# Shorter score tiles for the early queries of a cross attention, and constants made later, in a one-core decoder layer

## The reference

```python
def _L0_xattn_ref(x, encoder_output, mask, WQ, WK, WV, WO):   # H = 16, DK = 8
    q, k, v = ...                                             # (b, h, 64, 8)
    scores = jnp.einsum('bhqd,bhkd->bhqk', q, k) / SQRT_DK
    future = jnp.triu(jnp.ones((s, s), jnp.int32), 1)
    m = mask[:, None, :, None] + future[None, None, :, :]     # the mask is by query
    scores = jnp.where(m != 0, NEG, scores)
    attn = jax.nn.softmax(scores, axis=-1)
    return jnp.einsum('bhqk,bhkd->bqhd', attn, v)... @ WO
x = _layernorm(x + _L0_attn_ref(x, ...))
x = _layernorm(x + _L0_xattn_ref(x, ctx_1024, mask, ...))
x = _layernorm(x + _L0_ffn_ref(x, ...))
```

## Time and profile before

| | us |
|---|---|
| median of 3 runs | 600.04 |
| lowest and highest | 596.92, 603.64 |
| the profiled execution | 602.87 |
| its span | 601.2 |
| busy: PE, DVE, ACT, POOL | 527.9, 416.3, 369.0, 330.8 |

### The profile page before, as it was taken

How to read it: one execution, slowest core, us unless ns; L and a number is a source line. 1 busy time by engine, 2 the same in 40 slices (tenths; PEclk the granted TensorE clock), 3 DMA queues, 4 the chain that set the end, 5 groups by cost and what they waited for, 6 DMA issues and landing times.

```text
span 601.2 us, 22996 instructions
## 1 busy us (share of the span) xinstructions
PE 527.9 (88%) x9312; PEld 370.4 (62%) x9312; DVE 416.3 (69%) x1453; ACT 369.0 (61%) x643; POOL 330.8 (55%) x603
## 2 busy tenths in 40 slices
PE   2699998989999999988999999998989989999741
PEld 1467776656677767755666666666646656666530
DVE  2567777766767765375587778777867787779743
ACT  2356566557777777766766666666656666666520
POOL 6766667745755556341337554655465447554563
PEclk9899999999999999999999999999999999999876
DMA  5610000000000001001112111111111011111001
GB/s 160 188 38 3 3 1 2 3 3 1 1 2 1 2 5 26 1 11 28 27 32 49 29 40 33 49 30 43 29 48 28 27 48 50 28 34 22 20 19 35
DMA packets 24986, 17.97 MB, mean 30 GB/s; under 512 B 3120, under 2 KB 21424, under 8 KB 24880
## 3 DMA queue, kind: packets, MB, share of 16 engines
q1 hardware_dynamic: 24448, 16.43, 10.4%
q10 hardware_dynamic: 432, 0.07, 0.1%
HBM read 9.67 MB, written 4.19 MB: 23 GB/s over the span
## 4 chain that ended last, share of the span: by engine, by line
PE 58%; SPq 9%; ACT 8%; DVE 7%; issue 7%; POOL 6%; DMA 4%; POOLq 0%; DVEq 0%; ACTq 0%
SPq L394 8%; PE pair L1145 7%; PE pair L1179 7%; PE pair L1194 6%; PE pair L1213 6%; PE pair L1258 5%; PE pair L1114 5%; PE pair L1223 4%; PE pair L1036 4%; DMA k_exp<-k_sb 3%; ACT gel L718 3%; PE pair L1107 3%; PE pair L1232 2%; PE pair L1201 2%; PE pair L1049 2%
## 5 line engine op out<-in xcount | busy, mean ns | idle before, releaser
L718 ACT ACTIVATE gel<-pair 128x1024 f32<-128x1024 f32 x64 | 65.5, 1024 | 75.4 <-PE pair L1213 75.4
L926 DVE TENSOR_REDUCE neg_max<-pair 128x16 f32<-128x1024 f32 x64 | 60.9, 951 | 20.3 <-PE pair L1201 20.2
L1194 PE MATMUL pair<-k_exp,qT 64*32 64x256 f32 (+1 forms) x1024 | 57.5, 501 | 8.5 <-DMA k_exp<-k_sb 7.7
L1179 PEld LDWEIGHTS pair<-w,gel 128*128 128x128 f32 x512 | 60.3, 192 | 7.4 <-issue 5.5
L1223 PEld LDWEIGHTS pair<-v,gel 128*32 128x32 f32 x4096 | 41.7, 110 | 37.1 <-ACT gel L718 31.2
L1179 PE MATMUL pair<-w,gel 128*128 128x128 f32 x512 | 62.2, 276 | 1.0 <-ACT gel L643 1.0
L1223 PE MATMUL pair<-v,gel 128*32 128x18 f32 x4096 | 48.2, 187 | 15.5 <-ACT gel L718 12.8
L1145 PE MATMUL pair<-hT,w 128*128 128x512 f32 x128 | 58.5, 597 | 1.9 <-ACT lev L638 1.3
L712 ACT ACTIVATE gel<-gel,row_scale 128x512 f32<-128x512 f32 x80 | 54.4, 719 | 4.8 <-DVE gel L939 4.8
L303 POOL TENSOR_SCALAR veps_c<-mv_c 128x4 f32<-128x4 f32 x16 | 3.7, 229 | 96.0 <-issue 89.8
L303 POOL TENSOR_SCALAR veps_b<-mv_b 128x4 f32<-128x4 f32 x32 | 7.8, 245 | 81.6 <-DVE mv_b L295 45.8
(11 more groups left out here) (127 smaller groups left out, 1228.5 us busy)
## 6 DMA issues: line engine op xcount, KB each, us to landing
X<-in_x SPq DMA_DIRECT2D x16, 256.0 KB, 3.0
cT<-in_ctx SPq DMA_DIRECT2D x16, 256.0 KB, 2.9
out_rows<-X SPq DMA_DIRECT2D x16, 256.0 KB, 2.5
k_exp<-k_sb SPq DMA_DIRECT2D x160, 16.0 KB
w<-in_L_attn_w SPq DMA_DIRECT2D x2, 256.0 KB, 3.3
w_kv<-in_L_attn_wk SPq DMA_DIRECT2D x1, 64.0 KB, 3.2
w_q<-in_L_attn_wq ACTq DMA_DIRECT2D x1, 64.0 KB, 3.0
w_kv<-in_L_attn_wv SPq DMA_DIRECT2D x1, 64.0 KB, 3.1
```

The costliest lines, as they stand in the source:

```text
L718: nc.scalar.activation(pT[par], pair[par][:, :, :].rearrange("p a c -> p (a c)"), ACT.Copy).then_inc(pT_ready, 1)
L926: nc.vector.tensor_reduce(neg_max[par][:, :].rearrange("p (a h) -> p a h", a=2), scores, AX.X, ALU.max, negate=True).then_inc(max_ready, 1)
L1179: last = nc.tensor.matmul(bank(6 + q)[:, P * t:P * (t + 1)], gel[:, q, f, P * t:P * (t + 1)], w_2[:, f, :], start=(f == 0), stop=(f == NF ...
L1194: nc.tensor.matmul(pair[t % 2][b * QW:(b + 1) * QW, half, 0:HH * width], qT[p][rows, batch + first:batch + first + QW], keys, start=True, ...
```

## The change

- Odd tiles keep 32 keys per head to the end: probabilities of 512 columns, four transposes in place of eight, a copy of 512 columns, then four products of 144 columns (a masked query's share of the later 32 keys, from `future` and `v2`) and sixteen of 36 columns, from a new array `v4`. The even tiles add the causal term for the last 32 keys only (256 columns in place of 512).
- `v4` is a second copy of the values, which POOL writes in each group: `spread_v`, four copies, between `ln_b` and `ln_c` of its step. POOL's two `future_keys` per group go.
- `future` is made by DVE, one instruction per group (new `future_keys`), from rows of the mask that SP loads two groups ahead with one more DMA per group (`load_mask`), between the ten of `spread_k` and the load of the context. Two such loads follow the first context load.
- POOL's constants of the cross attention move from between `rows1` of groups 1 and 2 in stage one to behind the two `zero`, ahead of step 2 of `phase2`; those for `v4` and `late_key` are added.
- At the start of the cross attention ACT does `probabilities(0)` ahead of `rows_a(13)`, and `rows_a(14)` and `rows_a(15)` stand one and two slots later. `y2` takes the memory of `xn[0]` and `causal` that of `y2T`.

```diff
+            def load_mask(g, p):
+                src = mask_early[2 * g:2 * g + 2, :].rearrange("n p -> (n p)")
+                sp.dma_start(mask_rows[p][:, :, :].rearrange("p n q -> p (n q)"),
+                             src.partition_broadcast(P)).then_inc(mask_loaded[p], 16)
...
                 if exists(s + 2):
+                    if s >= 0:
+                        sp.wait_ge(future_ready, s + 1)
+                        load_mask(s + 2, p)
                     after(sp, xv_done, s + 1)
                     load_ctx(s + 2, p)
...
+            def late_constants():
+                const(nc.gpsimd.memset(causal, 0.0))
+                const(nc.gpsimd.memset(late_key[:, :], 0.0))
...
+                for i in range(2):
+                    const(nc.gpsimd.memset(v2[i][:, :, :, :, :], 0.0))
+                    for h in range(2):
+                        const(nc.gpsimd.memset(v2[i][h * S:(h + 1) * S, :, :, h, DH:HV], 1.0))
+                    const(nc.gpsimd.memset(v4[i][:, :, :, :, :], 0.0))
+                    for j in range(QB):
+                        const(nc.gpsimd.memset(v4[i][j * QW:(j + 1) * QW, :, :, j, DH:HV], 1.0))
+                    const(nc.gpsimd.memset(moe_out[i][:, :, 2 * D + NE:], LOWEST))
+                pool.sem_inc(const_ready)
...
-            def future_keys(m):
...
+            def spread_v(g, q):
+
+                pool.wait_ge(v2_ready, g + 1)
+                apart(pool)
+                heads = v2[q].rearrange("p u (i j) h e -> p u i j h e", j=2)
+                for j in range(2):
+                    for h in range(2):
+                        slot = 2 * j + h
+                        nc.gpsimd.tensor_copy(
+                            v4[q][slot * QW:(slot + 1) * QW, :, :, slot, 0:DH],
+                            heads[h * S:h * S + QW, :, :, j, h, 0:DH]).then_inc(v4_ready, 1)
+                        pool.wait_ge(v4_ready, g * QB + slot + 1)
...
             for s in range(2):
                 zero(k_exp[s])
 
+            late_constants()
             pipeline(pool, phase2, first=2, last=NG - 4)
...
-                nc.scalar.activation(pT[par], pair[par][:, :, :].rearrange("p a c -> p (a c)"),
-                                     ACT.Copy).then_inc(pT_ready, 1)
+                flat = pair[par][:, :, :].rearrange("p a c -> p (a c)")
+                nc.scalar.activation(pT[par], flat[:, 0:GW] if n % 2 else flat, ACT.Copy)\
+                    .then_inc(pT_ready, 1)
...
+            probabilities(0)
             rows_a(NG - 3, 1)
-            probabilities(0)
+            act.wait_ge(down_done, NG)
+            phase3(0, 0, slots=(0, 1))
             rows_a(NG - 2, 0)
-            act.wait_ge(down_done, NG)
-            phase3(0, 0, slots=(0,))
+            phase3(0, 0, slots=(2,))
             rows_a(NG - 1, 1)
-            phase3(0, 0, slots=range(1, TG))
+            phase3(0, 0, slots=(3,))
...
+            def future_keys(g, q):
+
+                dve.wait_ge(mask_loaded[q], g // 2 * 16 + 16)
+                after(dve, pv_done, g * TG - TG)
+                nc.vector.tensor_scalar(future[q][:, :, :], mask_rows[q][:, :, :], 0.0,
+                                        late_key[:, 0:1], ALU.not_equal, ALU.mult)\
+                    .then_inc(future_ready, 1)
...
-                for i in range(HH):
+                for i in range(HH // 2 if n % 2 else HH):
...
+                if n % 2:
+                    pe.wait_ge(v4_ready, (n // TG + 1) * QB)
+                    pe.wait_ge(future_ready, n // TG + 1)
+                    for b in range(QB):
+                        nc.tensor.matmul(
+                            bank(7)[b * QW:(b + 1) * QW, 0:H * HV],
+                            future[p][:, t // 2, b * QW:(b + 1) * QW],
+                            v2[p][:, t // 2 * QB + b, :, :, :].rearrange("p i h e -> p (i h e)"),
+                            start=True, stop=False)
+                    for i in range(QB):
+                        for b in range(QB):
+                            last = nc.tensor.matmul(
+                                bank(7)[b * QW:(b + 1) * QW, QB * HV * i:QB * HV * (i + 1)],
+                                pT[1][:, P * i + b * QW:P * i + (b + 1) * QW],
+                                v4[p][:, t // 2 * QB + b, i, :, :].rearrange("p h e -> p (h e)"),
+                                start=False, stop=i == QB - 1)
+                    last.then_inc(pv_done, 1)
+                    return
```

More of the change, by code:

```diff
@@ L89, in decoder_layer @@
         row_scale = sb("row_scale", [P, NT])
-        row_masked = sb("row_masked", [P, NT])
+        late_key = sb("late_key", [P, 1])
+        mask_rows = [sb(f"mask_rows{i}", [P, 2, P], I32) for i in range(2)]
+        future = [sb(f"future{i}", [P, 2, P]) for i in range(2)]
         ident = sb("ident", [P, P])
@@ L138, in decoder_layer @@
         v2 = [sb(f"v2{i}", [P, 2 * TG, HH, 2, HV]) for i in range(2)]
+        v4 = [sb(f"v4{i}", [P, 2 * TG, QB, QB, HV]) for i in range(2)]
         neg_max = [sb(f"neg_max{i}", [P, H]) for i in range(2)]
-        y2 = sb("y2", [P, TG, D])
+        y2 = xn[0]
         y2T = sb("y2T", [P, GW])
+        causal = y2T[:, :].rearrange("p (h k) -> p h k", k=S)
         moe_out = [sb(f"moe_out{i}", [P, TG, 2 * D + TOPW]) for i in range(2)]
@@ L220, in decoder_layer @@
         kexp_loaded = [sem(f"kexp_loaded{i}") for i in range(2)]
-        xv_done, v2_ready = sem("xv_done"), sem("v2_ready")
+        xv_done, v2_ready, v4_ready = sem("xv_done"), sem("v2_ready"), sem("v4_ready")
+        mask_loaded = [sem(f"mask_loaded{i}") for i in range(2)]
         s_done, max_ready, sub_ready, exp_ready = (sem(n) for n in
@@ L381, in _ @@
             load_ctx(0, 0)
+            load_mask(0, 0)
+            load_mask(1, 1)
             def spread_k(g, q):
@@ L434, in rows2 @@
                              lambda t: xn[p][:, t, :], mv[p], negm, rstd[p])
+            def late_constants():
+                const(nc.gpsimd.memset(causal, 0.0))
+                const(nc.gpsimd.memset(late_key[:, :], 0.0))
+                const(nc.gpsimd.memset(half_mask[:, :], 1.0))
+                for b in range(2):
+                    m = half_mask[b * S:(b + 1) * S, :]
+                    const(select(out=m, in_=m, compare_op=ALU.is_ge, fill=0.0, base=0,
+                                 pattern=[[-DH, HH]], channel_multiplier=1))
+                    const(select(out=m, in_=m, compare_op=ALU.is_ge, fill=0.0, base=DH - 1,
+                                 pattern=[[DH, HH]], channel_multiplier=-1))
+                    const(nc.gpsimd.memset(late_key[b * S + QW:(b + 1) * S, :], 1.0))
+                    c = causal[b * S:(b + 1) * S, :, :]
+                    const(select(out=c, in_=c, compare_op=ALU.is_ge, fill=NEG, base=S - QW,
+                                 pattern=[[0, HH], [-1, S]], channel_multiplier=1))
+                for i in range(2):
[7 more added lines that the diff above has]
+                pool.sem_inc(const_ready)
             select = nc.gpsimd.affine_select
@@ L454, in _ @@
                 rows1(i, i)
[L455 to L473, removed]
             def phase1(s, p):
@@ L559, in _ @@
             phase2(NG - 3, 1)
+            spread_v(0, 0)
             phase2(NG - 2, 0)
@@ L994, in phase3 @@
                 for t in slots:
+                    if t == 2 and exists(s + 1):
+                        future_keys(s + 1, q)
                     if exists(s) if t < TG - 1 else exists(s + 1):
@@ L1198, in scores @@
                     rows = slice(half * FH, half * FH + QW)
-                    future = causal_bf[rows, :].rearrange("p (h k) -> p h k", k=S)[:, :, S - width:]
+                    newer = causal_bf[rows, :].rearrange("p (h k) -> p h k", k=S)[:, :, QW:]
                     for b in range(QB):
-                        last = nc.tensor.matmul(pair[t % 2][b * QW:(b + 1) * QW, half, 0:HH * width],
-                                                ident_bf[rows, rows], future,
-                                                start=False, stop=True)
+                        row = pair[t % 2][b * QW:(b + 1) * QW, half, 0:HH * width]
+                        last = nc.tensor.matmul(
+                            row.rearrange("p (h k) -> p h k", k=width)[:, :, width - QW:],
+                            ident_bf[rows, rows], newer, start=False, stop=True)
                 last.then_inc(s_done, 1)
```

50 lines of the change are left out of this document (18 added, 32 removed).

## The result

| | before | changed |
|---|---|---|
| median of the runs, us (number of runs) | 598.48 (4) | 607.45 (4) |
| lowest and highest | 596.90, 603.64 | 604.63, 610.28 |
| ratio, with its 95% interval | 1 | 1.0135 (1.0088 to 1.0181) |
| the profiled execution, and its span | 602.87, 601.2 | 604.63, 602.9 |
| busy: PE, DVE, ACT, POOL | 527.9, 416.3, 369.0, 330.8 | 514.6, 418.8, 356.2, 342.4 |

A second set of runs of the same two kernels, on one chip, gave 599.51 and 604.26: 1.0101 (1.0064 to 1.0137). So the change costs 5 to 9 us, about 1%. PE's busy time fell by 13.3 us (mostly the transposes of odd tiles: all transposes of probabilities took 70.6 us before and 57.2 after), and the kernel is no faster for it.

What follows compares the result with a forecast made beforehand. Two close bounds in cross attention: PE near 19.1 us per group, the loop of DVE, POOL, SP and DMA at 19 to 20. Terms -4.8 + 13.7 - 3.3 - 2.8 - 2.5 = +0.3 on median 600.04 gave 600.3, range 593 to 611.

Steps and rivals of the forecast that it cites:

- The prediction's own case: Whole kernel: the forecast of 600.3 us holds, with its own range 595 to 606, chance 0.64.
- rivals at 606 to 612: Cross attention: clock drops in nearly all groups, 610, chance 0.11; mask DMA or late `spread_v`, 606 to 612, chance 0.07.
- Feed-forward, +13.7: Feed-forward: POOL's moved constants (11.8 us) delay DVE's deviation and stall PE, which restarts at low clock; 13.7 us lost.
- Stage one, -4.8: Stage one: without the constants PE's 2.60 us wait and 2.24 us of low-clock products go; 4.8 us won.
- Loop, -3.3: Cross attention, 12 groups: loop of DVE, POOL, SP and DMA shortens the period from 19.9 to 19.3; 3.3 us won.
- First two groups, -2.8: Cross attention's first two groups: no mixture, so no such loop, and PE's savings come through; 2.8 us won.
- Tail, -2.5: Tail from 548.16: shorter transposes, causal terms, copy and last odd tile, no further spread; 2.5 us won.
- Edits taken at nothing: Cross attention: `spread_v`, `load_mask` and both engines' `future_keys` edits are covered by other work or on no path; 0 us.
- The rule weighed: Feed-forward: DVE and POOL instructions exclude each other on a shared port; meetings of 0.24 us could make +13.7 into +14.3.
- the one that put the constants at no cost: Feed-forward: the constants are hidden and cause no stall, 586.6 us; chance 0.09.
- the loop isn't what binds: Cross attention: DVE and POOL have room, so the period falls to PE's 17.5, 575 us, or halfway, 586; chance 0.09.
- slower by the clock: Cross attention: PE's wait before slot 3's scores grows to 1.8 us, clock falls in nearly each group, 610 us; chance 0.11.

Runs made afterwards that it cites:

- second pair: Second profiles of both kernels, nothing altered: the changed kernel profiled at 605.80 us, the kernel before at 599.97.
- e10: The kernel before, nothing altered, run again for a profile near its median: 598.69 us, profiled at 599.97.
- e4: The kernel before with SP's store of a group moved one step later, behind the ten key DMAs: 590.69 us, ratio 0.9877.
- e3: The changed kernel with SP's store of a group moved one step later, behind the ten key DMAs: 594.03 us, ratio 0.9935.
- e6: Changed kernel with constants in six parts and the later store, plus DVE's future rows moved behind the attention rows of slot 2: 581.31 us, ratio 0.9719.
- e2: The changed kernel with POOL's constants cut into six parts, one in each of steps 3 to 8 of the feed-forward: 595.82 us, ratio 0.9937.
- first pair: First profiles of both kernels: the changed kernel profiled at 604.63 us, the kernel before at 602.87.

## Why the prediction was right, and where it was wrong

The range held the time (607.45 in 593 to 611), and the mechanisms of both large terms were right. The prediction's own case (595 to 606, chance 0.64) did not hold it; the wider range did, as it took in the rivals at 606 to 612 whose mechanisms didn't come. The forecast itself, no change, was 7 us too low (4 in the second set): at 1.0135 and 1.0101 the kernel lies at or just past the 1% that was called slower, a case that had a chance of 0.21. Of the 5.6 us between the sum's +0.3 and the +5.9 of the second pair, stage one makes 3.1, the tail 2.0 and the loop 1.9, less 1.4 from the feed-forward and the stretch to scores 2. By the steps of the sum:

- **Feed-forward, +13.7.** Right, 12.4 to 12.7. The constants took 11.5 us (11.8 said), for the reason given: they stand ahead of the deviation that DVE wants. That PE restarts at the low clock was right, at 2.5 us or less: the gap itself is 11.41, then the first trace lost 1.34 us on 16 products and 0.5 on the transposes, less some overlap. In the second trace the low clock lasted into the next up projection (4.25 in place of 3.60), 0.65 us more, which the table has in its next row.
- **Stage one, -4.8.** The mechanism was right (no wait for POOL's rows, `hT` copies 6.87 apart from the start: 24.56, 31.43, 38.29), the size was wrong, and this is the largest part of the miss. The 2.24 us "in which PE's products ran at the low clock after that wait" were taken from starts of pieces of the chain; by the timeline the `hT` copies start at 26.09, 35.07 and 41.93, which gives 2.12. And they were a property of the execution that was profiled, not of the kernel: e10 and e4 have the wait without them, and a shorter wait. What the change wins against e10 is 1.7. The changed kernel's first trace is 0.62 us later than its second from the start on: its `kv` projection at 13.6 took 3.62 in place of 2.95 (1.99 in the next group, at the full clock), so PE ran longer at the low pace of its start. The step that failed is the one at the end of the sum: the terms were made against the profiled 602.87 and then subtracted from a median 2.8 us lower, which already lacked the stretch that the term gave back.
- **Loop, -3.3.** The loop is the one named, shown by e3. 10.41 + 0.51 + 6.66 + 1.44 stand where 10.4 + 0.5 + 6.8 + 1.6 were said. Three low-clock stretches, as said. Of the gain 1.4 to 3.7 arrived, for the same reason as above: the 19.9 of the first trace is 19.78 in another. PE's wait for the keys was to pass 20 us and is 14.2 + 1.4; part of the rest is DVE's new wait of 13 x 0.28 = 3.6, which the prediction didn't name.
- **First two groups, -2.8.** Right: -2.5 and -2.9.
- **Tail, -2.5.** Wrong, -0.5. The last odd tile's transposes gave their 0.9 (1.11 against 1.97). What was not seen is that PE then waits for DVE:

```profile
567.28 1.01 PE L1271 MATMUL pair<-v,gel 128*32 128x18 f32 x64 [2.38 <-DVE att L937]
...
571.16 0.71 PE L1255 MATMUL pair<-v,future 128*32 128x144 f32 x8
...
572.28 2.99 PE L1306 MATMUL pair<-w_moe,y2T 128*128 128x263 f32 x8
```

1.5 us of that wait stood there before as well. And the mean granted clock of the tail is 0.73 in place of 0.78, so that the weighing takes 572.28 - 571.16 = 1.1 us and not 0.68.
- **Edits taken at nothing.** All held. `spread_v` is 4 x 0.41 (within 0.24 to 1.30), and POOL still stands 3.96 us ahead of `ln_c`. The mask's DMA issues in 0.45 us while SP has nothing else. The weighing is 0.68 against 0.67. Only DVE's future rows (0.34) were taken as covered by the saved time of PE: with the store ahead the closed loop doesn't pass through them, with the store behind the chain does (e3, e6).
- **The rule weighed.** The four memsets of 1152 columns took 1.06 each: DVE stood and waited all the time, so there was no meeting. The Trainium skill (SBUF — State Buffer, on the port that DVE and GpSimd share) says that of two such instructions the one that starts first keeps the port to its end and the other one waits. The traces of stage one agree: POOL lost 0.24 us where DVE was first, DVE lost 0.8 to 0.9 where POOL was first (e10, e4). So the prediction's 0.24 us per meeting was the cheaper of the two outcomes. In e2 such memsets ran beside DVE's statistics and sums that read `pair` and still took 1.05 and 1.06, so not every company costs.

The rivals: the one that put the constants at no cost was wrong for this kernel and right for e2; "the loop isn't what binds" was wrong; slower by the clock was wrong in its mechanism, since the number of drops is three, as said. The sign came out slower by no rival's mechanism: the cost in the feed-forward was as forecast, and the gains beside it were 10.7 us in the first pair and 6.8 in the second, where 13.4 was forecast.

## What to carry to other kernels

Work that moves to an idle engine is priced by what stands behind it in that engine's order. Here 11.5 us cost 12.4 in one piece ahead of a wanted deviation, and nothing in six pieces behind it. When PE's own work shrinks and the time doesn't, walk the closed loop from one wait of PE to the next: here one store ahead of ten DMAs in SP's order was worth 10 to 12 us in the changed kernel and 7 in the one before. And a term that gives back a low-clock stretch must be taken off the time of an execution that has it, so profile the kernel before twice when the sum hangs on one.

## What the runs showed of the hardware

- A low-clock stretch isn't tied to the length of the wait ahead of it alone. After 2.60 us in stage one PE's transposes took 1.12, after 1.65 us 0.66. In the changed kernel a wait of 2.41 us ahead of the scores was followed by scores of 1.26, and one of 1.41 by 1.96; in e10 one of 2.53 us was followed by scores of 1.09, the full clock.
- Which of two instructions starts first decides who pays. DVE's of 0.43 us, begun 0.12 us ahead of POOL's memset of 1.06, made that 1.30; begun 0.13 us behind it, it took 1.21 itself (e10).
- Small products: 64 with 18 columns took 0.67 us from start to start at the full clock; 8 with 144 and 32 with 36 took 0.68 together, though they are 40 in place of 64 and have twice the columns.
- The future rows, a comparison of 128 x 256 whole numbers into f32 with a second operation, took 0.34 us on DVE and 1.19 on POOL (two other operations with the same values).
